# Local attention in a two-layer megakernel: value products of two units paired in every second step, probabilities scaled before their transposes

## The reference

```
qkv = shift_token(x) @ wqkv                      # 8 heads of 64
q, k = l2norm(q) * qs, l2norm(k) * ks; rotary
sim = (8 q) k^T over this window of 128 and the one before (256 keys), masked
attn = softmax(sim);  out = attn @ v
x = x + out @ wo
h = layernorm(shift_token(x)) ...; x = x + (a * gelu(g)) @ w2 + b2   # hidden width 682
```

## Time and profile before

| | |
|---|---|
| median of 3 runs | 2962.12 us (2961.7 to 2962.24) |
| the profiled execution's own time | 2961.06 us |
| its span | 2959.0 us |
| busy share PE / DVE / ACT / POOL | 96% / 75% / 80% / 56% |
| chain of work that ended last, by engine | PE 90%, DVE 3%, ACT 2%, POOL 2% |
| mean granted TensorE clock | 0.984 |

### The profile page before, as it was taken

One profiled execution on the slowest core, in us unless ns is written; L12 is line 12 of the kernel. 1 busy time (PEld: TensorE's weight loads), 2 busy tenths in 40 slices (PEclk: granted clock), 3 DMA queues, 4 the chain that ended last, 5 costly groups with the idle time before them and its releaser, 6 DMA issues.

```text
span 2959.0 us, 67980 instructions
## 1 busy us (share of the span) xinstructions
PE 2839.2 (96%) x23460; PEld 2582.5 (87%) x23460; DVE 2208.8 (75%) x6587; ACT 2366.8 (80%) x5429; POOL 1643.3 (56%) x1652
## 2 busy tenths in 40 slices
PE   7999938999999999999999999999999999999987
PEld 6878826799999989999999999999999999999987
DVE  3979967778777777787777777777777777777763
ACT  4989946788888888888888888888888888888873
POOL 2323225666666666666666555666666666666643
PEclk9999968999999999999999999999999999999999
DMA  3152111111111111111110212111111111111000
GB/s 97 62 180 76 39 57 38 34 41 40 34 41 36 38 36 40 41 40 38 36 41 27 68 41 88 33 34 33 33 34 33 34 34 34 33 34 32 29 19 30
DMA packets 139624, 132.16 MB, mean 45 GB/s; under 512 B 16402, under 2 KB 134932, under 8 KB 138260
## 3 DMA queue, kind: packets, MB, share of 16 engines
q1 hardware_dynamic: 139284, 127.82, 14.2%
HBM read 77.33 MB, written 42.05 MB: 40 GB/s over the span
## 4 chain that ended last, share of the span: by engine, by line
PE 90%; DVE 3%; ACT 2%; POOL 2%; issue 2%; SPq 1%; DMA 1%; POOLq 0%; DVEq 0%; ACTq 0%
PE ps L385 50%; PE ps L359 10%; PE ps L469 8%; PE ps L455 7%; PE ps L443 7%; PE ps L428 4%; PE ps L479 2%; PE ps L405 1%; PE ps L497 1%; ACT Sm L730 1%; POOL rs L1200 1%; PE ps L346 1%; PE ps L534 1%; PE ps L533 0%; SPq L1383 0%
## 5 line engine op out<-in xcount | busy, mean ns | idle before, releaser
L730 ACT ACTIVATE Sm<-Sm,nb,sc 128x256 f32<-128x256 f32 (+1 forms) x1024 | 597.6, 588 | 2.2 <-DVE nb L1061 1.4
L1054 DVE CUSTOM_DVE_ANT_0 Sm<-ps,mask 128x256 f32<-128x256 f32 (+1 forms) x1024 | 368.3, 415 | 79.5 <-PE ps L443 77.3
L1127 DVE SCALAR_TENSOR_TENSOR Gl<-ps,vecs,Gl 128x256 f32<-128x256 f32 (+1 forms) x384 | 173.3, 479 | 317.5 <-ACT Gl L774 161.0
L385 PE MATMUL ps<-zTh,W1h 128*128 128x256 f32 (+1 forms) x1408 | 405.3, 288 | 0.0
L385 PE MATMUL ps<-zTl,W1h 128*128 128x256 f32 (+1 forms) x1408 | 397.4, 282 | 0.0
L385 PE MATMUL ps<-zTh,W1l 128*128 128x256 f32 (+1 forms) x1408 | 393.1, 279 | 0.0
L1200 POOL TENSOR_TENSOR rs<-rs,mhalf 128x16 f32<-128x16 f32 x128 | 372.3, 2909 | 0.0
L710 ACT ACTIVATE sq<-ps 128x512 f32<-128x512 f32 x256 | 152.5, 596 | 254.6 <-PE ps L385 254.1
L1291 POOL TENSOR_TENSOR uTl<-Gl,uTh 128x512 fp32r<-128x512 f32 (+1 forms) x192 | 211.0, 1105 | 254.6 <-ACT uTh L784 202.0
L385 PE MATMUL ps<-WQh,hTh 128*128 128x512 f32 x768 | 341.9, 445 | 2.8 <-DVE hTl L1011 2.8
L385 PE MATMUL ps<-WQl,hTh 128*128 128x512 f32 x768 | 305.0, 397 | 0.0
(11 more groups left out here) (188 smaller groups left out, 8982.4 us busy)
## 6 DMA issues: line engine op xcount, KB each, us to landing
tb<-tab SPq DMA_DIRECT2D x128, 128.0 KB, 2.3
xc<-x SPq DMA_DIRECT2D x32, 256.0 KB, 3.1
rwkv_scratch<-rw SPq DMA_DIRECT2D x32, 256.0 KB, 2.6
rk<-rwkv_scratch SPq DMA_DIRECT2D x64, 128.0 KB, 2.3
xin<-x SPq DMA_DIRECT2D x64, 128.0 KB, 2.2
x_scratch<-x SPq DMA_DIRECT2D x64, 128.0 KB, 1.7
y_scratch<-os SPq DMA_DIRECT2D x64, 128.0 KB, 4.1
y<-y_scratch SPq DMA_DIRECT2D x64, 128.0 KB, 4.0
```

The lines of the kernel that those rows point to most:

```text
L385: ins = pe.matmul(dst, L(a), R(b), start=start and i == 0, stop=stop and i == 2)
L730: act.activation(Sm[:, h, c0:c1_], Sm[:, h, c0:c1_], ACT.Exp, bias=nb[:, h:h + 1], scale=sc[:, n % 4, h:h + 1], accum_out=sm[:, n % 2, h:h ...
L1054: dve.tensor_tensor_reduce(Sm[:, h, c0:c1_], PS[:, bank["scores", n, q, h % 2], (h // 2 % 2) * 256 + c0:(h // 2 % 2) * 256 + c1_], mask[:, ...
L1127: dve.scalar_tensor_tensor(out=Gl[0:v, j % 4, :], in0=s, scalar=V("b1a", 6 * l + j, 0, v), in1=gl, op0=ALU.add, op1=ALU.mult).then_inc(S[" ...
```

## The change

The probabilities are scaled by 1/sum in Sm before their transposes: VectorE takes the reciprocals of four heads at a time (`p_sums`), GpSimd multiplies heads 0 to 3 (`p_norm`, first in its step) and VectorE heads 4 to 7 (`p_norm`, behind `z_stats`). `turn_p` waits for these in place of the exponentials. The spread, its transpose, `rT_out`, `o_norm` and the tile oF go; `oT_hi` and `oT_lo` read the value product from PSUM. The value products of units t-6 and t-5 are done together behind the scores of every odd t (the w2 steps); PT and oT have two buffers for this.

```diff
-    if live(6):
-        yield "rT", t - 6
-        yield "pv", t - 6
     if live(7):
         yield "wo", t - 7
...
@@ -128,6 +125,11 @@
         yield "scores", t - 4, 0, 1
         yield "scores", t - 4, 1, 0
         yield "scores", t - 4, 1, 1
+    if t % 2:
+        if live(6):
+            yield "pv", t - 6
+        if live(5):
+            yield "pv", t - 5
...
-        PT = sb("PT", [8, 256])
+        PT = sb("PT", [2, 8, 256])
-        rob = sb("rob", [8, 64])
-        oF = sb("oF", [4, 128])
-        oT = pair("oT", [4, 128])
+        oT = pair("oT", [2, 4, 128])
...
             if what == "pv":
-                return S["on"], n + 1
+                return S["oTl"], n + 1
...
             def turn_p(n, j):
                 c0, c1_ = cols(n)
                 k = bank["turn", n, j]
-                w.wait_ge(S["ex"], 8 * n + 2 * j + 2)
+                if j < 2:
+                    w.wait_ge(S["pn0"], n + 1)
+                else:
+                    w.wait_ge(S["pn1"], n + 1)
                 w.wait_ge(*read_out(former["turn", n, j]))
...
-                                            PT[:, 2 * c + par, s * 128:(s + 1) * 128],
+                                            PT[:, n % 2, 2 * c + par, s * 128:(s + 1) * 128],
...
-            def turn_r(n):
-                k = bank["rT", n]
-                w.wait_ge(S["rob"], n + 1)
-                w.wait_ge(*read_out(former["rT", n]))
-                for c in range(4):
-                    ins = pe.transpose(PS[:, k, c * 128:(c + 1) * 128],
-                                       rob[:, 2 * c:2 * c + 2, :].rearrange("p h d -> p (h d)"), ident[:, :])
-                ins.then_inc(S["p7"], 1)
...
                 odd = 1 - t % 2
-                if live(6):
-                    turn_r(t - 6)
-                    pv(t - 6, 0)
-                    pv(t - 6, 1)
                 if live(7):
                     wo_mm(t - 7)
                 if live(10) and not odd:
...
                 if live(4):
                     scores(t - 4, 0)
                     scores(t - 4, 1)
+                if live(6) and not odd:
+                    pv(t - 6, 0)
+                    pv(t - 6, 1)
+                if live(5) and not odd:
+                    pv(t - 5, 0)
+                    pv(t - 5, 1)
                 if live(2):
...
             def exp(n, q):
                 c0, c1_ = cols(n)
                 w.wait_ge(S["nb"], 2 * n + q + 1)
-                w.wait_ge(S["ro"], n - 1)
+                w.wait_ge(S["ro"], 2 * (n - 2) + q + 1)
...
-                w.wait_ge(S["p6"], 2 * (n - 1) + j // 2 + 1)
-                act.activation(PT[:, 2 * j:2 * j + 2, c0:c1_],
+                w.wait_ge(S["p6"], 2 * (n - 2) + j // 2 + 1)
+                act.activation(PT[:, n % 2, 2 * j:2 * j + 2, c0:c1_],
 
-            def rT_out(n):
-                w.wait_ge(S["p7"], n + 1)
-                w.wait_ge(S["oTl"], n)
-                act.activation(flat(oF[:, :, :]), PS[:, bank["rT", n], :], ACT.Copy).then_inc(S["rT"], 1)
-
             def oT_hi(n):
-                w.wait_ge(S["on"], n + 1)
-                w.wait_ge(S["p8"], n)
-                act.activation(flat(oT[0][:, :, :]), flat(oF[:, :, :]), ACT.Copy).then_inc(S["oTh"], 1)
+                w.wait_ge(S["p6"], 2 * n + 2)
+                w.wait_ge(S["p8"], n - 1)
+                act.activation(flat(oT[0][:, n % 2, :, :]), PS[:, bank["pv", n], :], ACT.Copy).then_inc(S["oTh"], 1)
...
                 odd = 1 - t % 2
-                if live(6):
-                    rT_out(t - 6)
                 if live(5):
                     exp(t - 5, 1)
...
                     gelu((t - 11) // 2, 2)
-                if live(6):
+                if live(6) and not odd:
                     oT_hi(t - 6)
+                if live(5) and not odd:
+                    oT_hi(t - 5)
                 if live(2):
...
-            def o_sums(n):
-                w.wait_ge(S["ex"], 8 * n + 8)
-                w.wait_ge(S["rob"], n)
-                dve.reciprocal(ro[:, :], sm[:, n % 2, :]).then_inc(S["ro"], 1)
-
-            def o_norm(n):
-                w.wait_ge(S["p6"], 2 * n + 2)
-                w.wait_ge(S["rT"], n + 1)
-                dve.tensor_tensor(flat(oF[:, :, :]), PS[:, bank["pv", n], :], flat(oF[:, :, :]),
-                                  ALU.mult).then_inc(S["on"], 1)
+            def p_sums(n, q):
+                r = slice(4 * q, 4 * q + 4)
+                w.wait_ge(S["ex"], 8 * n + 4 * q + 4)
+                if q:
+                    w.wait_ge(S["pn1"], n)
+                else:
+                    w.wait_ge(S["pn0"], n)
+                dve.reciprocal(ro[:, r], sm[:, n % 2, r]).then_inc(S["ro"], 1)
+
+            def p_norm(n):
+                c0, c1_ = cols(n)
+                w.wait_ge(S["ro"], 2 * n + 2)
+                dve.tensor_tensor(Sm[:, 4:8, c0:c1_], Sm[:, 4:8, c0:c1_],
+                                  ro[:, 4:8].unsqueeze(2).broadcast_to([128, 4, c1_ - c0]), ALU.mult).then_inc(S["pn1"], 1)
 
             def oT_lo(n):
                 w.wait_ge(S["oTh"], n + 1)
-                w.wait_ge(S["p8"], n)
-                dve.tensor_tensor(flat(oT[1][:, :, :]), flat(oF[:, :, :]), flat(oT[0][:, :, :]).bitcast(F32),
+                w.wait_ge(S["p8"], n - 1)
+                dve.tensor_tensor(flat(oT[1][:, n % 2, :, :]), PS[:, bank["pv", n], :], flat(oT[0][:, n % 2, :, :]).bitcast(F32),
                                   ALU.subtract).then_inc(S["oTl"], 1)
...
                 odd = 1 - t % 2
                 if live(1) and t - 1 < NG:
                     pre_y(t - 1)
+                if live(5):
+                    p_sums(t - 5, 0)
                 if live(9):
                     z_norm(t - 9)
                 if live(8):
                     z_stats(t - 8)
-                if live(6):
-                    o_norm(t - 6)
+                if live(5):
+                    p_sums(t - 5, 1)
+                    p_norm(t - 5)
                 if live(7):
                     x2_out(t - 7)
                     zero_h2(t - 7)
...
-                if live(6):
+                if live(6) and not odd:
                     oT_lo(t - 6)
-                if live(5):
-                    o_sums(t - 5)
+                if live(5) and not odd:
+                    oT_lo(t - 5)
                 if live(2):
                     rope(t - 2, 1)
...
-            def spread(n):
-                w.wait_ge(S["ro"], n + 1)
-                w.wait_ge(S["p7"], n)
-                pool.tensor_copy(rob[:, :, :], ro[:, :].unsqueeze(2).broadcast_to([128, 8, 64])).then_inc(S["rob"], 1)
+            def p_norm(n):
+                c0, c1_ = cols(n)
+                w.wait_ge(S["ro"], 2 * n + 1)
+                pool.tensor_tensor(Sm[:, 0:4, c0:c1_], Sm[:, 0:4, c0:c1_],
+                                   ro[:, 0:4].unsqueeze(2).broadcast_to([128, 4, c1_ - c0]), ALU.mult).then_inc(S["pn0"], 1)
 
...
+                if live(5):
+                    p_norm(t - 5)
                 if live(8):
                     root1(t - 8)
...
-                if live(5):
-                    spread(t - 5)
                 if live(2):
```

More of the change, by code:

```diff
@@ L297, in read_out @@
                 return S["x2"], n + 1
-            if what == "rT":
-                return S["rT"], n + 1
             if what == "zT":
@@ L488, in wo_mm @@
                 for c in range(4):
-                    ins = mm3(PS[:, k, 0:256], lambda a: oT[a][:, c, :], lambda a: WO[a][:, c, :], c == 0, c == 3)
+                    ins = mm3(PS[:, k, 0:256], lambda a: oT[a][:, n % 2, c, :], lambda a: WO[a][:, c, :], c == 0, c == 3)
                 ins.then_inc(S["p8"], 1)
```

## The result

The changed kernel takes 3553.37 us (median of 4 runs, 3548.97 to 3555.27) against 2961.98 for the kernel before, run beside it: a ratio of 1.1995 (95% interval 1.1974 to 1.2015), 592 us slower. The forecast was 3535 us, slower, by waits of TensorE for GpSimd's product and by the clock behind them.

What follows compares the result with a forecast made beforehand. The prediction took TensorE to bound the kernel. From 2961 us, less 68 saved, plus 485 of waits (together +417) and 158 of clock loss, it reached 3536, say 3535 us, range 3350 to 3650.

Steps and rivals of the forecast that it cites:

- What TensorE waits for, and how long: At turn_p(0), TensorE waits for GpSimd's product of heads 0 to 3 in every step, 485 us in sum.
- the four kinds of step: Waits at turn_p(0): second layer w2 4.8 us, MLP 1.75; first layer w2 5.4, MLP 3.4.
- E: End of the third qkv part, where turn_h starts; ScalarE's value copy and the exponentials behind it can't start earlier.
- The product's 1.9 us: GpSimd's 128x1024 product, estimated as twice L1269's 1.04 us less a fixed 0.2.
- The clock: TensorE's clock falls behind the long waits, costing 1.7 us in each of 93 steps, 158 us.
- What TensorE saves: turn_r's 0.53 us per step goes, 1.06 us per pair, 68 us over 64 pairs.
- Parts counted at nothing: Heads 4 to 7, paired pv, oT_lo, x2_out, scale, DMAs and other engines' lists: covered, no cost.
- cover of 1.5 us: Second layer's w2 step: VectorE's product ready by 10.3 us after E, turn_p(2) asking at 11.8.
- The rival of a faster kernel (2893 us): At turn_p(0), GpSimd's product ready by 4.2 us after E, no wait, 68 us gained; chance 0.04.
- The rival of no clock loss (3378): Waits at turn_p(0) come, but TensorE's clock stays up, 3378 us; chance 0.20.
- The rival of the blocked second half (3625): VectorE and GpSimd block each other, turn_p(2) 1.4 us late, 90 us on top, 3625 us; chance 0.12.
- The signs in the profile: turn_p heads TensorE's waits, 128 times, some 480 us; pairs 50 and 45 us, busy about 83%, clock near 0.94.

Runs made afterwards that it cites:

- e2: Changed kernel with 42 identity transposes ahead of turn_p(0)'s wait in w2 steps, 20 in the first layer's MLP steps: 3394.04 us, ratio 1.1458.
- e14: e11 with GpSimd's scale ahead of the root of z's variance, and VectorE's first GLU product or x3_out ahead of z_norm and z_stats: 2946.34 us, ratio 0.9947.
- e1: Changed kernel, but turn_p's first half takes raw exponentials and GpSimd's product goes into an unread tile: 3431.28 us, ratio 1.1583.
- e10: Changed kernel, but both halves of turn_p take raw exponentials and both engines' products go into unread tiles: 3329.52 us, ratio 1.1241.
- e13: e10 with x2_out moved to the head of VectorE's step: 3249.51 us, ratio 1.0974.
- e9: e8 with the second half started early too: exp(t-4, 1) in ScalarE's tail, VectorE's product of heads 4 to 7 ahead of hT_lo: 3202.52 us, ratio 1.0812.
- e11: e9 with hT_lo ahead of VectorE's product and oT_lo and x2_out first in the step, value products separate: 3182.88 us, ratio 1.0746.
- e12: e11 with the value products of two units paired, as in the change: 3250.65 us, ratio 1.0976.
- e8: Changed kernel with value products one unit per step and the first half early (exp(t-4, 0) ahead of v_out, reciprocals and GpSimd's product earlier): 3184.36 us, ratio 1.0751.

## Why the prediction was right, point by point

- **What TensorE waits for, and how long.** The forecast gave 4.8, 1.75, 5.4 and 3.4 us for the four kinds of step; steady steps of the profile after show 5.02, 1.67, 5.39 and 3.32. Over all units 496 us against 485. TensorE's idle time rose by less, 474 us (119.8 to 594.1), since waits of before went with turn_r and the raw exponentials (11.5 and 7.2 us). That each wait begins anew at E holds less well in the first layer: in a steady w2 step turn_p went on 10.36 us after E, but 11.02 in e2, where TensorE's clock brings E sooner and VectorE's list doesn't follow. The product's 1.9 us, taken from the product with a broadcast operand nearest to it, measured 1.875. An estimate from the Trainium skill (GPSIMD Engine Reference, section Performance versus the Vector engine) had been 2.2 us and more; the measurement decides for the row.
- **The clock.** The forecast was 158 us. Filling the waits gave back 159 (e2). By the sum, 3553 - 2959 + 68 - 496 leaves 166. That TensorE idled and its clock then fell to the lower level is thus both seen and undone. The size was luck in two ways. The earlier trace rows are headed as the longest idle time of the drain, but two longer ones stand there: 4.05 us, ended at 2876.94 and followed by a clock of 0.72 as well, and 3.91 us, followed by a lower one:

```profile
2896.43 0.90 PE L479 MATMUL ps<-ident,rob 128*128 128x128 f32 x3 [3.91 <-POOL rob L1277]
...
2896.50:2902.50 6.00, 6.00 (x45) 5.34 (x46) 1.40 (x5) 0.60 (x1) 1.11 (x2) 0.57 0.00 0
```

  From this last row (clock 0.57, third from the end) the same working gives 5.2 us at the lower level, 2.6 us lost, and 93 x 2.6 = 240 us. And 3.4 us at the lower level, costing half of that, is not what happened. A mean clock of 0.916 over 3553 us is 597 us at the lower level, and 0.983 over 3393 us in e2 is 115: 482 us less, or 5.2 per filled wait, gave back 159 us, a third of it and not half. Part of these 482 us lies in the waits themselves. Too short a time at too high a price made the right 1.7 us.
- **What TensorE saves.** This term, 68 us, was too large. e14 is the one kernel in which TensorE is busy throughout in the second layer, and its pairs there are 0.6 to 0.7 us shorter than before (2195.84 to 2233.02 is 37.18 against 37.82), not 1.06. Part of turn_r's 0.53 us comes back in the turn to the value products: from turn_h to pv it takes 0.31 us (2212.86 to 2213.17 in e14), where turn_h to turn_r took 0.22, and the transposes of P ahead of the second w2 product take 0.95 us where they took 0.79. With 64 x 0.64 = 41 us in its place, the residual above would leave 139 us for the clock and not 166; with the 474 us of idle time in place of 496 as well, it leaves 161, close to e2's 159. So the forecast's terms were off by 27 us (saving), -11 (waits) and 3 (clock), 19 in all: 3536 + 19 is 3555, the profiled execution's own time.
- **Parts counted at nothing.** Here the forecast held for the changed kernel, and for the reason given: its cover of 1.5 us was reckoned behind TensorE's own wait for GpSimd (8.95 + 2.87). What it did not say is that the cover goes with the wait. e1 took the wait away, and 323 us of waits for VectorE's product appeared; e10 and e13 found x, the exponentials, Gl and os in the same shadow. The waits for hTl and oTl in e9 and for Ar in e11 are of another kind: the new order of the lists made them.
- **The rival of a faster kernel (2893 us)** therefore had more in its way than the forecast said. It would have needed GpSimd's product by 4.2 us after E, and also places in the lists for a second product, for x2_out and for the power. e14 has all of these, with separate value products and exponentials ahead of v_out, and reaches 2946.
- **The rival of no clock loss (3378)** is what e2 makes of it: 3394. In the changed kernel itself it did not occur.
- **The rival of the blocked second half (3625)** did not cost time: 0.9 us of waits for VectorE's product. Its mechanism is in the trace, with the roles turned round. A root of one element on GpSimd takes 1.62 us where VectorE's product runs beside it (2336.19, above), and 0.55 where VectorE reads from PSUM (e11, above). The Trainium skill says that the two share a port pair, that one holds it for its whole instruction while the other blocks, and that VectorE needs it with two inputs in SBUF or in a two-port mode (SBUF — State Buffer, section SBUF: two separate sides). By that rule, the trace agrees.
- **The signs in the profile** came as named: turn_p's line at the head of the waits, 128 times, 496 us (480 or so), pairs of 51.2 and 45.5 us (50 and 45), busy share 83% (83%), a clock of 0.916 over the whole span (0.94, a little too high).

What stays open: the paired products with e14's lists were not run. By e12 less e11 they would cost about 68 us there, an estimate. The pairing without the scaling was not run either, nor e14's two moves apart, so which of them gave how much is open. Of e14's 237 us, 189 are idle time of TensorE (327.9 in e11, 139.3 here); the other 48 are busy time of the same 22948 instructions at the same mean clock, and why is not shown.

## What to carry to other kernels

Moving work off the busiest engine also moves the moment at which it asks for the next thing. Here the 1.9 us of value products in front of the transposes were cover, and taking them away cost 324 us of the 592 with no work added. A wait that shows in a profile hides the ones behind it: VectorE's product, x, the exponentials, Gl and os came up here, one after the other, so "waited for 0.9 us" is no slack. The same scaling went from 592 us slower to 15 faster, by undoing the pairing and by giving every entry of three in-order lists a place at which its input is there and nobody needs what stands behind it.

## What the runs showed of the hardware

Some instructions of GpSimd and VectorE hold each other up, in both directions, until the other's ends. The first two of e1's rows from 1368.64 on, above, show it: VectorE's normalization z of 128x128 (its like takes 0.34 us in the earlier trace rows) starts 0.07 us behind GpSimd's product and ends with it, after 1.92 us.

Others don't. In the changed kernel VectorE's reciprocal of 128x4 keeps its 0.18 us beside GpSimd's product, and x2_out, which reads PSUM, its 0.42 us beside the power (2315.54, with the power from 2314.87 for 3.52).

The hold-up shows over all units too, and goes with the place of GpSimd's product in its list. The same z takes 1.43 us on average in the changed kernel and 0.34 in e14. In e8, where the product comes early, another small VectorE instruction meets it: the one of 16 elements that makes rs takes 0.87 us on average, in the changed kernel 0.24. First z, in the changed kernel and in e14, then rs, in e8 and in the changed kernel:

```profile
L1107 DVE TENSOR_SCALAR z<-h,mv,r 128x128 f32<-128x128 f32 x128 | 183.4, 1433 | 0.0
```

```profile
L1099 DVE TENSOR_SCALAR z<-h,mv,r 128x128 f32<-128x128 f32 x128 | 43.3, 338 | 0.0
```

```profile
L1020 DVE TENSOR_SCALAR rs<-ss 128x16 f32<-128x16 f32 x128 | 110.8, 866 | 4.4
```

```profile
L1028 DVE TENSOR_SCALAR rs<-ss 128x16 f32<-128x16 f32 x128 | 30.6, 239 | 4.4
```

The power of rs on GpSimd, in turn, is 2.91 us on average in e8 and 3.37 in the changed kernel, where VectorE's product falls on its start in MLP steps (product from 2314.40 for 1.23 us, power from 2314.87 for 3.52). The clock was the other point: behind the waits of 3.3 us and more TensorE worked at its lower level for a while, which cost about 1.7 us a time (159 us over the 93 waits that e2 filled), and idle transposes during the wait prevented it. The loss did not grow with the length of the wait. In the changed kernel's first layer the wait of 5.39 us that ended at 1362.82 was followed by the first of these stretches, the wait of 3.32 us that ended at 1387.21 by the second (the clock is third from the end):

```profile
1363.00:1369.00 6.00, 6.00 (x47) 5.83 (x48) 3.02 (x9) 2.28 (x4) 5.09 (x3) 0.76 0.08 12
1387.50:1393.50 6.00, 6.00 (x31) 6.00 (x31) 2.95 (x8) 2.66 (x5) 5.12 (x4) 0.53 0.04 9
```
